# Two context attentions: the row sums of the softmax made in the spare half of each value tile, and divided through 32 transposed columns

## The chip, the cores and the metric

The kernel is one program on one core of a Trainium2 chip. The core has a matmul engine (PE; its weight loads are shown apart as PEld), three elementwise engines (DVE is VectorE, ACT is ScalarE, POOL is GpSimd) and a queue that only issues DMAs (SP). PE writes into PSUM, a memory of eight banks of 512 float32 columns by 128 partitions; the other engines read it from there. Each engine works through its own list in order and waits on semaphores for the others. The metric is the device time of one execution in microseconds.

## The reference

The program is a decoder of four layers over x of 8 sequences x 256 tokens x 256 features, with twelve stages; after each stage x is added to the stage's output and normalised. Two of the twelve (the second stage of layers 2 and 3, called stages 7 and 10 here) attend from x to a context of 77 rows per sequence, with 16 heads of width 16:

```python
q = (x @ Wq + bq).reshape(b, l, H, D).transpose(0, 2, 1, 3)
k = (context @ Wk + bk).reshape(b, s, H, D).transpose(0, 2, 1, 3)
v = (context @ Wv + bv).reshape(b, s, H, D).transpose(0, 2, 1, 3)
attn = jnp.einsum('bhld,bhsd->bhls', q, k) / jnp.sqrt(jnp.float32(D))
attn = jax.nn.softmax(attn, axis=-1)
out = jnp.einsum('bhls,bhsd->bhld', attn, v)
out = out.transpose(0, 2, 1, 3).reshape(b, l, E)
return out @ Wp + bp
```

Both have this form (the second with its weights transposed). All in float32.

## The kernel before

`cross16` builds both stages. Everything of a stage is pipelined over i = 0 to 11, with one sequence b entering at each i from 0 to 7, and the order of the work is written out by hand in the loop `for i in range(B + 4)` of each engine. For one sequence the steps are: queries (L296); scores of each half of the tokens, with the tokens on the partitions (L324), whose row maxima DVE takes (L504); the maxima transposed (L333) and sent by a DMA into one row of the padded queries; scores again, now with the 77 context rows on the partitions (L347, minus the maximum by that row), in two groups t = 0 and 1 of eight heads; their exponentials by ACT (L458); the product with the values (L361), for each t; the division (L511 and L513); the output projection (L377); residual sum and statistics (L520, L523, L526), the normalisation (L532), and x transposed for the next stage (L386, copied by ACT at L468).

Both kinds of scores use the same four banks, S.R. So within one i the sequence of their users is fixed: scores of the first half, maxima, scores of the second half, maxima, transposed scores t = 0, exponentials, transposed scores t = 1, exponentials, and then the next i. On PE the product of sequence i - 2, t = 1, stands between the two halves of the scores, and the product of sequence i - 1, t = 0, between the last transposed scores of i and the first scores of i + 1.

The heads' outputs are 16 wide, while PE writes 32 partitions for one group of columns of the array. So two heads share 32 partitions: v2 holds each head's values in one half of 32 columns (half s) and zeros in the other, and the two heads of a pair are added up in one bank, S_num. The row sums go the same way into a second bank, S_den, by a product with `ones2`, a tile that has ones in one half and zeros in the other (L365). Each matmul in float32 shows as two records in the trace, so a product of 8 matmuls is "x16". DVE takes the reciprocal of all of S_den (512 columns) and multiplies.

`keep_warm` (L212) issues matmuls whose result nobody reads, in places where PE has little to do; in these stages at i = 0 to 2 and from i = 10 on.

Of the kernel before, what the change touches and what calls it, by code (L numbers as in the profile page):

```python
# [12 lines left out]
ALU = mybir.AluOpType  # L13
ACT = mybir.ActivationFunctionType
AX = mybir.AxisListType

P = 128
B = 8
T = 256
# [8 lines left out]
CTX = 77  # L28
EPS = 1e-5
MASKED = -1e30  # L30
BANK = 512
# [23 lines left out]
def columns(parts):  # L55

    at, out = 0, {}
    for name, n in parts:
        out[name] = (at, n)
        at += n  # L60
    return out


CONST = columns([("ident", 128), ("causal", 128), ("causal_t", 128), ("block", 128), ("tri", 128), ("ones", 128),
                 ("steps", 256), ("past", 256), ("iota", 16), ("neg_half", 16), ("half", 64), ("row", 1),
                 ("head", HT), ("line_head", H), ("even", 1), ("odd", 1), ("sel", 3 * H), ("count", P)])
# [24 lines left out]
def part(image, table, name, chunks=None):  # L91

    at, n = table[name]
    v = image[:, at:at + n]
    return v.rearrange("p (c n) -> p c n", c=chunks) if chunks else v
# [93 lines left out]
def prefetch(nc, S, sp, k):  # L189

    if k < len(PACK):
# [8 lines left out]

Marks = namedtuple("Marks", "setup pads v_sb v_full k_full k_sb k_dma q_full q_sb q_dma s_full max_done neg_full neg_sb "
                            "neg_dma st_full exp_done pv_full attn_ready y_full yn_ready yt_full xt_done ln_stat "
                            "rstd_ready xres_ready y_read c_in c_stat c_rstd cn_ready cnt_sb first_done x_done xa_done xd_done xa_full "
                            "xd_full t_full pt_dve pt_act o_full rec_ready rows_ready recb_sb lat_stat lat_rstd lat_ready spare_free qb_done yb_done qa_full qd_full ya_full "
                            "yd_full feat_ready kg_ready line_ready lam_exp "
                            "setup_bc g_done prod_done state_done state_used diag_done odd_full odd_sb d_done raw_sb")
# [8 lines left out]
def settle(engine, mark, total):  # L215

    engine.wait_ge(mark, total)
    engine.sem_inc(mark, -total)
# [12 lines left out]
def cross16(nc, S, k, scale, first):  # L231
# [4 lines left out]
    W, TB, M = S.arena[k % 2], PACK[k], S.marks  # L236
    used = sum(n for _, n in TB.values())
    NK = B * CTX
    with ExitStack() as ctx:
        def sb(name, shape, dt=F32):  # L240
            return ctx.enter_context(nc.sbuf_tensor(f"{name}_{k}", shape, dt))

        v2 = W[:, used:used + B * H * 32].rearrange("p (b h m) -> p b h m", b=B, h=H)
        k_pad = W[:, used + B * H * 32:used + B * H * 32 + 4 * NK].rearrange("p (c n) -> p c n", c=4)
        prob_t = sb("prob_t", [P, C, 4, 2, T])
# [4 lines left out]
        rec = sb("rec", [P, C * T])  # L250
        attn_t = sb("attn_t", [P, 2, C, T])
# [2 lines left out]
        bst = sb("bst_own", [P, 2, TT, 6])  # L254
        mv = sb("mv_own", [P, 2, TT, 2])
        rstd = sb("rstd_own", [P, 2, TT])
        ones2 = sb("ones2", [P, 2, 32])
        bq_s = sb("bq_s", [P, C])
        S_q, S_y, S_num, S_den = S.T[:, 0, :], S.T[:, 1, :], S.O[:, 0, :], S.O[:, 1, :]

        def bank(j):
            return S.R[:, j // 2, j % 2 * BANK:(j % 2 + 1) * BANK]
# [24 lines left out]
        def _(pe):  # L287
# [64 lines left out]
            def product(b, t):  # L352
                pe.wait_ge(M.exp_done, 2 * b + t + 1)
                if t == 0:
                    if b == 0:
                        pe.wait_ge(M.v_sb, B // 2)
                    else:
                        pe.wait_ge(M.attn_ready, b)
                for s in range(2):
                    for j in range(4):  # L360
                        nc.tensor.matmul(S_num[32 * j:32 * j + 32, t * T:(t + 1) * T], v2[0:CTX, b, 8 * t + 2 * j + s, :],  # L361
                                         prob_t[0:CTX, t, j, s, :], start=(s == 0), stop=(s == 1), skip_group_check=True)
                for s in range(2):
                    for j in range(4):
                        last = nc.tensor.matmul(S_den[32 * j:32 * j + 32, t * T:(t + 1) * T], ones2[0:CTX, s, :],  # L365
                                                prob_t[0:CTX, t, j, s, :], start=(s == 0), stop=(s == 1), skip_group_check=True)
                if t == 1:
                    last.then_inc(M.pv_full, 1)

# [68 lines left out]
            settle(pe, M.neg_dma, 16 * B)  # L438
            settle(pe, M.exp_done, 2 * B)
            settle(pe, M.attn_ready, B)  # L440
            settle(pe, M.yn_ready, B)
            settle(pe, M.xt_done, B)

        @block.scalar
        def _(act):
            bk_even, bk_odd = part(W, TB, "bk_even"), part(W, TB, "bk_odd")
            even, odd = part(S.const, CONST, "even"), part(S.const, CONST, "odd")

            def queries(b):
                act.wait_ge(M.q_full, b + 1)  # L450
                for t in range(C):
                    last = nc.scalar.activation(q_pad[:, b % 3, 2 * t, :], S_q[:, t * T:(t + 1) * T], ACT.Identity,
                                                bias=bq_s[:, t:t + 1], scale=scale)
                last.then_inc(M.q_sb, 1)

            def exps(b, t):
                act.wait_ge(M.st_full, 2 * b + t + 1)
                nc.scalar.activation(prob_t[0:CTX, t, :, :, :].rearrange("p j s q -> p (j s q)"),  # L458
                                     S.R[0:CTX, :, :].rearrange("p a n -> p (a n)"), ACT.Exp).then_inc(M.exp_done, 1)

            def maxima(b):
                act.wait_ge(M.neg_full, b + 1)
                nc.scalar.activation(neg_t[:], S_q[0:H, 0:T], ACT.Copy).then_inc(M.neg_sb, 1)

            def transposed(b):
                act.wait_ge(M.yt_full, b + 1)
                y = S_y if b < B - 1 else S_q
                nc.scalar.activation(S.x_t[:, :, b * T:(b + 1) * T], y.rearrange("p (c t) -> p c t", c=C), ACT.Copy)\  # L468
                    .then_inc(M.xt_done, 1)

            act.wait_ge(S.weights_ready[k], 16)
            for t in range(C):
                act.wait_ge(M.k_full, t + 1)
                nc.scalar.activation(k_nat[:, t, :], S.R[:, t, 0:NK], ACT.Identity, bias=bk_odd[:, t:t + 1], scale=odd).then_inc(M.k_sb, 1)
            act.wait_ge(M.setup, 1)
            queries(0)
            for t in range(C):
                nc.scalar.activation(k_pad[:, 2 * t, :], S.R[:, t, 0:NK], ACT.Identity, bias=bk_even[:, t:t + 1], scale=even)\
                    .then_inc(M.k_sb, 1)
            for i in range(B + 4):  # L480
                if i + 1 < B:
                    queries(i + 1)
                if 0 <= i - 4 < B:
                    transposed(i - 4)
                if 0 <= i - 1 < B:
                    exps(i - 1, 0)
                if i < B:
                    maxima(i)
                if 0 <= i - 1 < B:
                    exps(i - 1, 1)  # L490
            settle(act, M.setup, 1)
            settle(act, M.q_full, B)
            settle(act, M.k_full, C)
            settle(act, M.st_full, 2 * B)
            settle(act, M.neg_full, B)
            settle(act, M.yt_full, B)

        @block.vector
        def _(dve):
            bv = part(W, TB, "bv")  # L500

            def maxima(b, qt):
                dve.wait_ge(M.s_full, 2 * b + qt + 1)
                nc.vector.tensor_reduce(neg_max[:, qt, :].rearrange("p (j c) -> p j c", j=4),  # L504
                                        S.R[:].rearrange("p a (e n) -> p (a e) n", e=2)[:, :, 0:4 * CTX]
                                        .rearrange("p j (c n) -> p j c n", c=4), AX.X, ALU.max, negate=True)\
                    .then_inc(M.max_done, 1)

            def quotient(b):
                dve.wait_ge(M.pv_full, b + 1)  # L510
                nc.vector.reciprocal(rec[:], S_den)  # L511
                dve.drain()
                nc.vector.tensor_tensor(attn_t[:, b % 2, :, :].rearrange("p c t -> p (c t)"), S_num, rec[:], ALU.mult)\  # L513
                    .then_inc(M.attn_ready, 1)

            def residual(b):
                dve.wait_ge(M.y_full, b + 1)
# [17 lines left out]

            dve.wait_ge(S.weights_ready[k], 16)
            nc.vector.tensor_scalar(bq_s[:], part(W, TB, "bq"), scale, None, ALU.mult).then_inc(M.setup, 1)
            nc.vector.memset(v2, 0.0)
            nc.vector.memset(ones2[:], 0.0)
            dve.drain()  # L540
            for s in range(2):
                nc.vector.memset(ones2[:, s, 16 * s:16 * s + 16], 1.0)

            def values(pair):
                dve.wait_ge(M.v_full, pair + 1)
# [26 lines left out]
            settle(dve, M.v_full, B // 2)  # L572
            settle(dve, M.s_full, 2 * B)
            settle(dve, M.pv_full, B)
            settle(dve, M.y_full, B)
            settle(dve, M.xres_ready, B)
            settle(dve, M.rstd_ready, B)
# [3903 lines left out]
def decoder(nc, dram, layers=range(12)):  # L4481

    with ExitStack() as ctx:
# [90 lines left out]
        with nc.Block() as block:  # L4574
# [33 lines left out]
            lambda k: moe_relu(nc, S, k),  # L4608
            lambda k: causal16(nc, S, k, D ** -0.5),
            lambda k: cross16(nc, S, k, DH16 ** -0.5, k == layers[0]),  # L4610
            lambda k: int8_product(nc, S, k),
            lambda k: selective_scan(nc, S, k),
# [120 lines left out]
```

## Time and profile before

| | |
|---|---|
| median of 3 runs | 3124.25 us (3118.69 to 3127.91) |
| the profiled execution, its own time | 3095.31 us |
| its span | 3093.5 us |
| PE busy | 2841.6 us, 92% of the span |
| DVE busy | 1909.1 us, 62% |
| ACT busy | 1199.2 us, 39% |
| mean granted clock of PE | 0.972 of full speed |
| stage 7 | about 2234 to 2371 us |
| stage 10 | about 2758 to 2891 us |

Times of rows are from the span's start. A timeline row gives start, duration, engine, line, operation, tiles, shape and count, and in brackets how long the engine had been idle before it and what released it. The duration of several merged instructions runs from the first start to the last end, and the ends on PE are modelled. The granted clock is either full (1.0, 2.4 GHz) or half (0.5, 1.2 GHz); a figure between them is a mean over the stretch.

### The profile page before, as it was taken

Reading aid. Unit: us, or ns where it says so; the run is one execution under the profiler, and the core shown is the slowest. Engines: PE = TensorE matmul, PEld = TensorE weight load, DVE = VectorE, ACT = ScalarE, POOL = GpSimd, SP = SyncE. Lnnn points to the kernel's source line nnn. Section 1 sums busy time; section 2 is a strip of 40 time slices with the busy share of each in tenths; the row PEclk is TensorE's granted clock in tenths of the full one; section 3 lists DMA queues with packets and bytes.
Section 4 is the critical chain, followed back from the end, with each engine's and each line's share of the span. In section 5 each row is a group of like instructions: output and inputs, shape, how many; then the busy total and the mean of one; then the engine's idle time right before and its main releaser. Section 6 shows DMA issues by size and latency. Waiting matters only on the chain. (4 is left out here: it accounts for less than half of the span.)

```text
span 3093.5 us, 55363 instructions
## 1 busy us (share of the span) xinstructions
PE 2841.6 (92%) x22416; PEld 1831.1 (59%) x22416; DVE 1909.1 (62%) x3404; ACT 1199.2 (39%) x2567; POOL 326.5 (11%) x460
## 2 busy tenths in 40 slices
PE   6999899999998978799999999989898899989898
PEld 3666456666666856466666667756565333346576
DVE  4666457777764335377777753345557999975532
ACT  1332245445542333254555432123232766634111
POOL 1111100000002700000000000100101000001232
PEclk9999999999999989899999999989999999999899
DMA  3001010000012231100000000000000000000241
GB/s 115 17 17 48 30 42 9 5 5 5 5 66 78 89 131 32 43 5 5 5 5 9 35 18 1 27 20 20 18 21 35 18 1 1 1 14 21 100 163 66
DMA packets 43418, 103.91 MB, mean 34 GB/s; under 512 B 4961, under 2 KB 32847, under 8 KB 39585
## 3 DMA queue, kind: packets, MB, share of 16 engines
q1 hardware_dynamic: 37377, 86.80, 8.1%
q0 software_dynamic: 5792, 13.59, 1.5%
q8 instruction: 182, 2.98, 0.4%
q14 instruction: 67, 0.55, 0.1%
HBM read 66.74 MB, written 19.07 MB: 28 GB/s over the span
## 5 line engine op out<-in xcount | busy, mean ns | idle before, releaser
L2388 ACT ACTIVATE prob<-R,neg_max 128x333 f32<-128x333 f32 x512 | 268.7, 538 | 184.1 <-DVE neg_max L2455 183.8
L3936 DVE TENSOR_TENSOR_SCAN arena<-arena,u 128x512 f32<-128x512 f32 x256 | 289.6, 1203 | 0.1
L2276 PEld LDWEIGHTS T<-const,prob 128*128 128x128 f32 (+1 forms) x1536 | 183.7, 143 | 82.1 <-DVE prob L2468 36.6
L2468 DVE TENSOR_TENSOR prob<-prob,rec 128x666 f32<-128x666 f32 x256 | 218.5, 853 | 20.2 <-issue 1.3
L2455 DVE TENSOR_REDUCE neg_max<-R 128x2 f32<-128x666 f32 x256 | 205.9, 846 | 35.2 <-PE R L2265 35.1
L2276 PE MATMUL T<-const,prob 128*128 128x128 f32 (+1 forms) x1536 | 210.9, 274 | 13.0 <-DVE prob L2468 10.7
L2395 ACT ACTIVATE prob_t<-T 128x384 f32<-128x384 f32 x256 | 125.8, 491 | 228.2 <-PE T L2276 222.1
L3867 ACT ACTIVATE arena<-delta,neg_a 128x510 f32<-128x510 f32 x256 | 175.4, 714 | 43.1 <-DVE arena L3936 42.0
L2461 DVE COPY prob_t<-T 128x384 f32<-128x384 f32 x256 | 142.3, 556 | 39.4 <-PE T L2276 13.0
L2195 PE MATMUL O<-keys_in,arena 128*128 128x333 f32 x512 | 164.8, 444 | 0.0
L3770 PE MATMUL R<-arena,diag 64*64 64x512 f32 x1024 | 134.7, 617 | 25.5 <-DVE arena L3936 25.4
L2191 PE MATMUL O<-keys_in,arena 128*128 128x256 f32 x512 | 127.7, 391 | 2.3 <-ACT keys_in L2361 2.3
L2202 PE MATMUL O<-arena,keys_in 128*128 128x512 f32 x256 | 125.1, 611 | 0.0
L2220 PE MATMUL O<-arena,attn_t 128*128 128x256 f32 x512 | 117.4, 382 | 1.0 <-DVE ysb L2438 1.0
L2191 PEld LDWEIGHTS O<-keys_in,arena 128*128 128x128 f32 x512 | 91.6, 189 | 37.1 <-issue 23.9
L944 DVE TENSOR_REDUCE neg_max<-R 128x8 f32<-128x2048 f32 (+1 forms) x24 | 55.0, 2292 | 94.5 <-PE R L721 94.5
L2220 PEld LDWEIGHTS O<-arena,attn_t 128*128 128x128 f32 x512 | 94.9, 190 | 19.8 <-issue 6.4
L2388 ACT ACTIVATION_READ_ACCUMULATOR prob<-R,neg_max 128x1 f32 x512 | 103.8, 203 | 0.0
L2195 PEld LDWEIGHTS O<-keys_in,arena 128*128 128x128 f32 x512 | 87.7, 191 | 24.0 <-issue 1.0
L2293 PE MATMUL O<-prob_t,v 128*64 128x256 f32 (+1 forms) x768 | 98.5, 392 | 1.3 <-DVE prob_t L2461 1.3
L2293 PE MATMUL O<-prob_t,arena 128*64 128x256 f32 (+1 forms) x768 | 97.2, 388 | 0.0
L3770 PEld LDWEIGHTS R<-arena,diag 64*64 64x64 f32 x1024 | 29.3, 133 | 112.9 <-DVE arena L3936 78.6
(597 smaller groups left out, 5390.1 us busy)
## 6 DMA issues: line engine op xcount, KB each, us to landing
w<-w_dram SPq DMA_DIRECT2D x16, 1024.0 KB, 7.0
arena<-pack_dram SPq DMA_DIRECT2D x2, 4100.0 KB, 15.2
q_pad<-q_pad SPq DMA_DIRECT2D x24, 224.0 KB, 2.7
arena<-pack_dram SPq DMA_DIRECT2D x4, 1284.0 KB, 6.5
arena<-pack_dram SPq DMA_DIRECT2D x1, 4896.0 KB, 14.6
slots_in<-x_nat SPq DMA_DIRECT2D x2, 2048.0 KB, 8.5
arena<-planes SPq DMA_DIRECT2D x8, 512.0 KB, 8.5
arena<-k_nat SPq DMA_DIRECT2D x16, 224.0 KB, 2.7
```

The source lines that it names most:

```text
L2191: last = nc.tensor.matmul(bank[:, h * T:(h + 1) * T], wq[:, c, (2 * i + h) * P:(2 * i + h + 1) * P], keys[:, c, CTX:XK], start=(c == 0), s ...
L2195: last = nc.tensor.matmul(bank[:, 0:XK], wkv[:, c, i * P:(i + 1) * P], keys[:, c, :], start=(c == 0), stop=(c == C - 1))
L2220: last = nc.tensor.matmul(bank[:, 0:D], attn_t[:, b % 2, c, i * P:(i + 1) * P], wo[:, c, :], start=(c == 0), stop=(c == HP - 1))
L2276: last = nc.tensor.transpose(S.T[0:n, i, kc * P:(kc + 1) * P], prob[:, g % 2, i, first:first + n], S.ident)
L2293: last = nc.tensor.matmul(S_o[XD * i:XD * (i + 1), 0:T], v[b % 2][0:n, kc, (2 * hp + i) * XD:(2 * hp + i + 1) * XD], prob_t[0:n, m % 2, i, ...
L2388: last = nc.scalar.activation(prob[:, g % 2, i, :], S.R[:, g % 2, i * BANK:i * BANK + XK], ACT.Exp, bias=neg_max[:, g % 2, i:i + 1], accum ...
L2455: nc.vector.tensor_reduce(neg_max[:, g % 2, :], S.R[:, g % 2, :].rearrange("p (i n) -> p i n", i=2)[:, :, 0:XK], AX.X, ALU.max, negate=Tru ...
L2461: nc.vector.tensor_copy(prob_t[:, m % 2, 0, :, qt * P:(qt + 1) * P], S.T[:, 0, 0:3 * P].rearrange("p (c q) -> p c q", c=3)).then_inc(M.pt_ ...
L2468: nc.vector.tensor_tensor(prob[:, g % 2, :, :], prob[:, g % 2, :, :], rec[:, g % 2, :].unsqueeze(2).to_broadcast([P, 2, XK]), ALU.mult)\
L3770: last = nc.tensor.matmul(sums(i, a)[to:to + HB, :], diag[rows, i % CT, n + a, :], state[rows, (q + a) % HELD, :], start=(a == 1 and n == ...
L3867: nc.scalar.activation(decay[:, q % DEEP, :].rearrange("p (b t) -> p b t", b=PAIR)[:, :, 1:T], delta[:, i % 2, :].rearrange("p (b t) -> p ...
L3936: nc.vector.tensor_tensor_scan(state[:, q % HELD, :], decay[:, q % DEEP, :], u[:, i % 2, :], 0.0, ALU.mult, ALU.add)\
```

## The change

Both heads of a pair no longer share a bank. v2 is filled with ones in place of zeros, so that each head's tile of 32 columns has its values in one half and ones in the other. The even head of a pair writes to one bank (S_one) and the odd head to the other (S_two), each by one matmul with no accumulation. On 32 partitions a bank then has 16 rows of the head's weighted values and 16 equal rows of its sums. `ones2` and the matmuls of L365 are gone: a product is 8 matmuls, not 16.

Putting the two heads together takes more steps on the elementwise engines. ACT copies S_one to SBUF, with `even` as a scale that sets the partitions of the sums to zero (`halves`). DVE transposes both banks in blocks of 32 x 32, adds the odd heads to ACT's copy (a scalar_tensor_tensor with the mask `odd`), takes the reciprocal of 32 columns, one for each block and bank, of the transposed tile, transposes these back with each repeated 16 times, and multiplies. PE may write the banks again after the sum (semaphore sums_read), where it had to wait for the whole division (attn_ready).

```diff
@@ product @@
                     if b == 0:
                         pe.wait_ge(M.v_sb, B // 2)
                     else:
-                        pe.wait_ge(M.attn_ready, b)
-                for s in range(2):
+                        pe.wait_ge(M.sums_read, b)
+                for s, sums in enumerate((S_one, S_two)):
                     for j in range(4):
-                        nc.tensor.matmul(S_num[32 * j:32 * j + 32, t * T:(t + 1) * T], v2[0:CTX, b, 8 * t + 2 * j + s, :],
-                                         prob_t[0:CTX, t, j, s, :], start=(s == 0), stop=(s == 1), skip_group_check=True)
-                for s in range(2):
-                    for j in range(4):
-                        last = nc.tensor.matmul(S_den[32 * j:32 * j + 32, t * T:(t + 1) * T], ones2[0:CTX, s, :],
-                                                prob_t[0:CTX, t, j, s, :], start=(s == 0), stop=(s == 1), skip_group_check=True)
+                        last = nc.tensor.matmul(sums[32 * j:32 * j + 32, t * T:(t + 1) * T], v2[0:CTX, b, 8 * t + 2 * j + s, :],
+                                                prob_t[0:CTX, t, j, s, :], start=True, stop=True, skip_group_check=True)
@@ scalar engine @@
+            def halves(b):
+                act.wait_ge(M.pv_full, b + 1)
+                if b >= 1:
+                    act.wait_ge(M.sums_read, b)
+                nc.scalar.activation(own[:], S_one, ACT.Copy, scale=even).then_inc(M.halves_sb, 1)
             for i in range(B + 4):
+                if 0 <= i - 2 < B:
+                    halves(i - 2)
                 if i + 1 < B:
                     queries(i + 1)
@@ vector engine @@
             def quotient(b):
                 dve.wait_ge(M.pv_full, b + 1)
-                nc.vector.reciprocal(rec[:], S_den)
-                dve.drain()
-                nc.vector.tensor_tensor(attn_t[:, b % 2, :, :].rearrange("p c t -> p (c t)"), S_num, rec[:], ALU.mult)\
-                    .then_inc(M.attn_ready, 1)
+                nc.vector.transpose(turned[:, 1, :], S_two)
+                dve.wait_ge(M.halves_sb, b + 1)
+                nc.vector.transpose(turned[:, 0, :], S_one)
+                shares = attn_t[:, b % 2, :, :].rearrange("p c t -> p (c t)")
+                nc.vector.scalar_tensor_tensor(shares, S_two, odd, own[:], ALU.mult, ALU.add).then_inc(M.sums_read, 1)
+                sums = turned[:].rearrange("p s n -> p (s n)")[:, 16:2 * BANK - 16].rearrange("p (s n) -> p s n", s=2)[:, :, 0:BANK - 31:32]
+                dve.drain()
+                nc.vector.reciprocal(inverse[:].rearrange("p n s -> p s n"), sums)
+                dve.drain()
+                nc.vector.transpose(rec[:].rearrange("p (n s m) -> p n s m", s=2, m=16), inverse[:].unsqueeze(3).to_broadcast([P, 16, 2, 16]))
+                dve.drain()
+                nc.vector.tensor_tensor(shares, shares, rec[:], ALU.mult).then_inc(M.attn_ready, 1)
@@ set-up @@
-            nc.vector.memset(v2, 0.0)
-            nc.vector.memset(ones2[:], 0.0)
-            dve.drain()
-            for s in range(2):
-                nc.vector.memset(ones2[:, s, 16 * s:16 * s + 16], 1.0)
+            nc.vector.memset(v2, 1.0)
+            dve.drain()
```

PE, stage 10, one pass of the loop in the middle of the pipeline (i = 4), before:

```order
L324 MATMUL R<-arena,q_pad 128x77 x16
L361 MATMUL O<-prob_t,arena 32x256 x8
L365 MATMUL O<-prob_t,ones_7 32x256 x8
L324 MATMUL R<-arena,q_pad 128x77 x16
L296 MATMUL T<-x_t,arena 128x256 x4
L386 MATMUL T<-const,x_nat 128x128 x4
L347 MATMUL R<-q_pad,arena 77x256 x8
L377 MATMUL T<-arena,attn_t 128x256 x4
L333 MATMUL T<-const,neg_max 16x128 x2
L347 MATMUL R<-q_pad,arena 77x256 x8
L361 MATMUL O<-prob_t,arena 32x256 x8
L365 MATMUL O<-prob_t,ones_7 32x256 x8
```

Now, the same pass (L324 of before is now L326, L361 is L363, and so on):

```order
L326 MATMUL R<-arena,q_pad 128x77 x16
L363 MATMUL O<-prob_t,arena 32x256 x8
L326 MATMUL R<-arena,q_pad 128x77 x16
L298 MATMUL T<-x_t,arena 128x256 x4
L384 MATMUL T<-const,x_nat 128x128 x4
L349 MATMUL R<-q_pad,arena 77x256 x8
L375 MATMUL T<-arena,attn_t 128x256 x4
L335 MATMUL T<-const,neg_max 16x128 x2
L349 MATMUL R<-q_pad,arena 77x256 x8
L363 MATMUL O<-prob_t,arena 32x256 x8
```

Two groups of 8 matmuls have gone; nothing else has moved on PE.

DVE, the same stage, the division in one pass, now (before, L511 RECIPROCAL of 128x512 and L513 TENSOR_TENSOR of 128x512 stood in this place, after the same two TENSOR_REDUCE):

```order
L519 STREAM_TRANSPOSE turned<-O 128x512
L521 STREAM_TRANSPOSE turned<-O 128x512
L523 SCALAR_TENSOR_TENSOR attn_t<-O,const,own 128x512
L526 RECIPROCAL inverse<-turned 128x2x16
L528 STREAM_TRANSPOSE rec<-inverse 128x512
L530 TENSOR_TENSOR attn_t<-attn_t,rec 128x512
L536 TENSOR_TENSOR ysb_own<-T,xres_own 128x512
```

Six instructions stand where two did. On ACT one more (L468 of the new kernel, own<-O, 128x512) stands ahead of the two copies of the queries in each pass from i = 2 to 9.

## Rows read from the trace of the kernel before

**Rows 1.** The page, busy time of the engines.
```profile
PE 2841.6 (92%) x22416; PEld 1831.1 (59%) x22416; DVE 1909.1 (62%) x3404; ACT 1199.2 (39%) x2567; POOL 326.5 (11%) x460
```

**Rows 2.** Groups by line and shape, PE: busy us, mean ns of one.
```profile
L365 PE MATMUL O<-prob_t,ones 77*32 77x256 f32 x512 | 33.5, 379 | 0.0
```

**Rows 3.** Timeline of stage 7, one pass of the loop (i = 6).
```profile
2321.37 1.07 PE L361 MATMUL O<-prob_t,arena 77*32 77x256 f32 x16
2321.50 1.44 DVE L504 TENSOR_REDUCE neg_max<-R 128x16 f32<-128x1232 f32 x1 [2.64 <-PE R L324]
...
2322.26 1.05 PE L365 MATMUL O<-prob_t,ones 77*32 77x256 f32 x16
...
2323.24 1.13 PE L324 MATMUL R<-arena,q_pad 16*128 16x77 f32 x32
...
2325.80 3.35 DVE L511 RECIPROCAL rec<-O 128x512 f32<-128x512 f32 x1
...
2329.22 0.69 DVE L513 TENSOR_TENSOR attn_t<-O,rec 128x512 f32<-128x512 f32 x1
...
2329.83 0.68 DVE L520 TENSOR_TENSOR ysb_own<-T,xres_own 128x512 f32<-128x512 f32 x1
...
2331.09 1.87 ACT L458 ACTIVATE prob_t<-R 77x2048 f32<-77x2048 f32 x1 [0.69 <-PE R L347]
...
2331.84 1.05 PE L365 MATMUL O<-prob_t,ones 77*32 77x256 f32 x16
...
2333.11 1.13 PE L324 MATMUL R<-arena,q_pad 16*128 16x77 f32 x32 [0.22 <-ACT prob_t L458]
...
2334.29 1.44 DVE L504 TENSOR_REDUCE neg_max<-R 128x16 f32<-128x1232 f32 x1 [2.64 <-PE R L324]
```

**Rows 4.** Stretches: us, busy (count) of PE, PEld, DVE, ACT, POOL, granted clock, DMA share, GB/s.
```profile
2270.20:2337.20 67.00, 65.06 (x994) 43.52 (x994) 44.60 (x49) 26.15 (x28) 9.24 (x16) 1.00 0.07 20
2337.20:2346.30 9.10, 8.03 (x46) 4.91 (x47) 6.84 (x6) 2.85 (x3) 0.00 (x0) 0.62 0.01 2
...
2860.40:2866.20 5.80, 4.73 (x46) 3.10 (x46) 5.72 (x4) 2.85 (x3) 0.00 (x0) 1.00 0.01 3
```

**Rows 5.** Timeline of stage 7 from the last maxima (i = 7) to the last transposes.
```profile
2337.23 1.44 DVE L504 TENSOR_REDUCE neg_max<-R 128x16 f32<-128x1232 f32 x1 [0.85 <-PE R L324]
...
2338.82 1.92 PE L347 MATMUL R<-q_pad,arena 17*77 17x256 f32 x16 [1.07 <-DVE neg_max L504]
...
2369.12 0.66 PE L386 MATMUL T<-const,x_nat 128*128 128x128 f32 x4
```

**Rows 6.** Timeline of stage 10, the same three instructions.
```profile
2860.41 1.44 DVE L504 TENSOR_REDUCE neg_max<-R 128x16 f32<-128x1232 f32 x1 [0.85 <-PE R L324]
...
2861.99 1.10 PE L347 MATMUL R<-q_pad,arena 17*77 17x256 f32 x16 [1.07 <-DVE neg_max L504]
...
2889.32 0.66 PE L386 MATMUL T<-const,x_nat 128*128 128x128 f32 x4
```

**Rows 7.** Timeline of stage 7, from i = 1 to i = 2.
```profile
2267.48 1.87 ACT L458 ACTIVATE prob_t<-R 77x2048 f32<-77x2048 f32 x1 [0.97 <-PE R L347]
...
2269.20 1.13 PE L212 MATMUL T<-ctx_t,const 128*128 128x512 f32 x2
2270.26 1.13 PE L324 MATMUL R<-arena,q_pad 16*128 16x77 f32 x32
```

**Rows 8.** Timeline of stage 10, the last division.
```profile
2877.36 1.57 DVE L532 TENSOR_SCALAR x_nat<-ysb_own,mv_own,rstd_own 128x256 f32<-128x256 f32 x2 [1.20 <-POOL rstd_own L597]
...
2879.22 3.36 DVE L511 RECIPROCAL rec<-O 128x512 f32<-128x512 f32 x1 [0.29 <-PE O L365]
```

**Rows 9.** Single lines: count, duration in ns (least/median/most), first and last start, form.
```profile
L468 ACT ACTIVATE x_t<-T x16: 598/599/600, 2301.5 to 2890.0; 128x512 f32<-128x512 f32 x16
L1925 DVE RECIPROCAL arena<-arena x8: 352/353/355, 45.6 to 279.8; 128x32 f32<-128x32 f32 x8
```

**Rows 10.** Groups by shape, 2200 to 2400 us: busy us, mean ns of one.
```profile
L3593 DVE TENSOR_SCALAR rows_i<-rows_i 128x512 f32<-128x512 f32 x5 | 2.1, 427 | 0.4
```

More of the change, by code:

```diff
@@ L202 @@
                             "neg_dma st_full exp_done pv_full attn_ready y_full yn_ready yt_full xt_done ln_stat "
-                            "rstd_ready xres_ready y_read c_in c_stat c_rstd cn_ready cnt_sb first_done x_done xa_done xd_done xa_full "
+                            "rstd_ready xres_ready y_read c_in c_stat c_rstd cn_ready cnt_sb first_done x_done xa_done xd_done halves_sb sums_read xa_full "
                             "xd_full t_full pt_dve pt_act o_full rec_ready rows_ready recb_sb lat_stat lat_rstd lat_ready spare_free qb_done yb_done qa_full qd_full ya_full "
@@ L256, in cross16 @@
         rstd = sb("rstd_own", [P, 2, TT])
-        ones2 = sb("ones2", [P, 2, 32])
+        own = sb("own", [P, BANK])
+        turned = sb("turned", [P, 2, BANK])
+        inverse = sb("inverse", [P, 16, 2])
         bq_s = sb("bq_s", [P, C])
-        S_q, S_y, S_num, S_den = S.T[:, 0, :], S.T[:, 1, :], S.O[:, 0, :], S.O[:, 1, :]
+        S_q, S_y, S_one, S_two = S.T[:, 0, :], S.T[:, 1, :], S.O[:, 0, :], S.O[:, 1, :]
         def bank(j):
@@ L440, in _ @@
             settle(pe, M.attn_ready, B)
+            settle(pe, M.sums_read, B)
             settle(pe, M.yn_ready, B)
@@ L500, in _ @@
             bv = part(W, TB, "bv")
+            odd = part(S.const, CONST, "odd")
             def maxima(b, qt):
@@ L574, in _ @@
             settle(dve, M.pv_full, B)
+            settle(dve, M.halves_sb, B)
             settle(dve, M.y_full, B)
```

## The prediction

> **What bounds the kernel now.** I read the page first, then the two stages as timelines, then stretches with the granted clock. The page has PE busy for 92% of the span [rows 1], which makes it look as if any matmul taken away were time gained. The removed matmuls, L365, are busy for 33.5 us in all [rows 2]. One pass of the loop says otherwise. It takes 2334.29 - 2321.50 = 12.79 us from one first maxima to the next [rows 3], and in it one chain through the shared banks S.R sets the time: scores, maxima on DVE, scores, maxima, transposed scores, exponentials on ACT, transposed scores, exponentials, scores. Both blocks of L365 stand beside a member of this chain that runs on another engine. The first (2322.26) lies beside the maxima of L504, which end at 2321.50 + 1.44 = 2322.94; the next scores start at 2323.24. The second (2331.84) lies beside ACT's exponentials, which end at 2331.09 + 1.87 = 2332.96; the next scores start at 2333.11, released by ACT. So PE is busy there, and nobody waits for what it does.
>
> DVE has the division (L511, 3.35 us, and L513, 0.69 us) after the second maxima, and waits 2.64 us for PE before the next pass [rows 3]. It is not the bound in the middle of a stage.
>
> The last thing to see is the clock. From 2270.20 to 2337.20, five full passes, PE is busy for 65.06 of 67.00 us at the full 2.4 GHz [rows 4]. Right behind, with the last maxima, PE had nothing to do for 1.07 us [rows 5], and in the stretch to 2346.30 the granted clock has a mean of 0.62: it fell to 1.2 GHz right after that gap. In stage 10 PE has the same gap of 1.07 us at the same place [rows 6], and the clock stays at 1.00 [rows 4]. So at this mix of work (scores on 16 rows of the array, a short idle time, transposes) a gap of about a microsecond brings the clock down in one of two cases. The price can be read off, as both stages run the same instructions: from L504 to the last L386 it is 2369.12 - 2337.23 = 31.89 us in stage 7 and 2889.32 - 2860.41 = 28.91 us in stage 10 [rows 5, 6], so one fall costs 2.98 us.
>
> **The change part by part.** All in the profiled execution, whose span is 3093.5 us and own time 3095.31.
>
> The matmuls that go. A block of L365 holds PE from 2322.26 to 2323.24, 0.98 us [rows 3].
> - Product t = 1, six passes a stage: without it the scores wait for DVE. After a release PE starts some 0.14 us later (2861.99 against 2860.41 + 1.44 = 2861.85 [rows 6]), so they start at 2323.08 and not 2323.24: 0.16 us each. What follows (queries, transposes, scores, projection) is PE's own unbroken work, so the gain is kept. 12 x 0.16 = 1.9 us.
> - Product t = 0 behind the last transposed scores: ACT sets the next scores, nothing. The exception is i = 1, where L212 stands behind it: the exponentials end at 2267.48 + 1.87 = 2269.35 and the scores start only at 2270.26 [rows 7]. Now 2269.49: 0.77 us in each stage, 1.5 us.
> - The end of a stage, where the last product and division are on the path. The last division starts at 2879.22, with the product before it and L532 (to 2877.36 + 1.57 = 2878.93) both just done [rows 8]. Both come earlier: the product by 0.98 us, L532 by what the earlier divisions and the earlier transposes give, which I take as 1.2 us.
>
> The division. Before: 3.42 to the start of the multiplication and 0.69, 4.11 us [rows 3]. Now six DVE instructions. An ordinary pass over 512 columns takes 0.69, and the next one starts 0.61 later (2329.22 to 2329.83) [rows 3]; a reciprocal of 32 columns takes 0.353 [rows 9]; a drain adds 0.07 (2325.80 + 3.35 to 2329.22). The transposes are in no row here. Their bounds are 0.43 us, the fastest pass over 512 columns [rows 10], and 3.35 us, the slowest (L511). I take 0.61 start to start, as they only move data. Sum: 3 x 0.61 for two transposes and the sum, 0.07, 0.35 + 0.07, 0.61 + 0.07, 0.69 = 3.7 us, 0.4 less. In the middle of a stage it is worth nothing, DVE has 2.64 us to spare; at the end of a stage it gives 0.4 once. With the 1.2 above 1.6 a stage, 3.2 us. With transposes at the lower bound 0.5 us less per division, at the upper bound see below.
>
> The Trainium skill has the transposes' price: "Vector Engine (DVE) Microarchitecture Reference", section 3.8, says the 32 x 32 reorder array is pipelined to one element per cycle and lane, so a transpose would cost what a copy does. No run so far shows it.
>
> ACT's copy of one bank: like L468, 0.60 us [rows 9]. It stands ahead of the queries' copies, at a time when ACT has just finished its exponentials and waits for PE. Behind it are the two copies that the DMA of the padded queries waits for, a whole pass ahead of their use. PE's queries come after the product on PE, so the copy is done before they are. Nothing.
>
> The waits. sums_read comes before attn_ready came, so PE waits no longer than before. ones2's memsets are gone from a start where DVE waits anyway. Nothing. No DMA is added or moved.
>
> So far -1.9 - 1.5 - 3.2 = -6.6 us.
>
> What the cover leaves behind. With L365 gone PE is idle in each pass twice: from about 2322.4 to 2323.1 beside the maxima, 0.6 us, and beside the exponentials from about 2332.0 to 2333.1, 1.1 us, with only 16-row scores and one small product in between. Both together exceed the gap of 1.07 us that brought the clock down in stage 7 [rows 5], and what lies between is thinner. It comes at the start of i = 3, 4, 5, 6 and 7 in both stages, and of i = 8 in stage 10 (stage 7 has that fall already): 11 places. The half clock would then lie on the part of the pass that is PE's alone (the second scores to the transposed scores t = 1, 2323.24 to about 2331), so nothing hides it. Bounds: no fall, 0; a fall at all 11, 11 x 2.98 = 33 us. I take 8 of 11, nearer to the upper end, as before one such gap in two was enough and now there are two in a row: 24 us.
>
> The Trainium skill has rules for both sides, in "TensorE: Matmul & The Clock Gate". Its section on HAM oscillation has the clock fall on long waits only, which would leave -6.6 us; the fall behind a 1.07 us gap speaks against it. The section on psum-queue depth-cycling says that micro-idles between groups of matmuls are enough for the clock to oscillate; the trace agrees once out of two.
>
> Sum: 24 - 6.6 = +17 us, about 3112 us in the profiled execution. That one is 29 us under the median of the runs (3124.25), so 3141 us for the median.
>
> **The rivals.**
> 1. The clock stays up. For it: stage 10 went through the same 1.07 us gap undisturbed, and five passes show not one fall. Against it: the new idle time is larger and returns in each pass. It gives -6.6 us: 3118.
> 2. PE's busy time is what counts, and the removed matmuls come off in full: -33.5 [rows 2] - 3 = 3088. For it: 92% busy, 65.06 of 67 us. Against it: both waits in rows 3 end on another engine. It would need the scores to start before the maxima or the exponentials are done.
> 3. DVE becomes the bound, through transposes that are slow on float32 or on PSUM. DVE has 2.64 us to spare in a pass; from a division of 4.11 + 2.64 = 6.75 us on it decides, that is transposes of 1.6 us each. At 3.35 each the division takes 12 us and a pass 5.2 us more: 12 passes, 62 us, 3186. For it: nothing in the trace shows such an instruction. Against it: plain passes over PSUM run at 0.69.
> Slower than before thus has two different ways, the clock and DVE; they can be told apart at once.
>
> **How the numbers follow.** What this kernel's measurement can tell from no change is about 0.3%, 9.4 us. Forecast, the clock falls in four passes or more (+5 to +33 us): 0.60, of which 0.52 is over +9.4. Rival 1: 0.24. Rival 2: 0.08. Rival 3: 0.08, nearly all of it over +9.4 us, 0.07. So slower 0.59, within 0.3% 0.29 (0.08 + 0.01 + 0.20 of rival 1), faster 0.12 (rival 2, and 0.04 of rival 1). The forecast's own range is 3129 to 3157. The whole range reaches to rival 1 with a little room, 3114, and to 3159.
>
> **What would show it.** In the profile after: L365's records gone; the scores behind the first product wait 0.1 to 0.2 us on DVE at a pass's start and PE's idle time before them is 0.6 us, and 1.1 us before those released by ACT; the division 3.7 us from first transpose to end; the granted clock of the middle of both stages clearly under 1.00, with passes of 15 to 16 us where it fell and of 12.6 where not. A clock of 1.00 in both stages makes rival 1 right. A pass of 10.8 us at full clock would be rival 2, a DVE without idle time before the first maxima rival 3. I am wrong if stages 7 and 10 together are not longer by 5 us or more, or if they are but at full clock.

## The result and the profile after

The changed kernel takes 3154.0 us (median of 7 runs, 3145.71 to 3168.41), the kernel before 3118.69 us (median of 7, the first three among them). The ratio is 1.0105, with a 95% interval of 1.0088 to 1.0122: slower by 1.05%, some 33 us. The forecast was slower, by 17 us. The profiled execution of the kernel before, 3095.31 us, on which the prediction's rows rest, is shorter than each of these seven (3111.51 to 3127.91).

The page of the changed kernel, busy time of the engines, answers to [rows 1]. 512 matmul records are gone and PE is busy for 31 us longer:

```profile
PE 2872.9 (91%) x21904; PEld 1850.1 (59%) x21904; DVE 1903.8 (60%) x3462; ACT 1209.4 (38%) x2583; POOL 325.5 (10%) x460
```

The five passes from the first maxima of i = 2 to those of i = 7, before, as stretches (columns as in [rows 4]), stages 7 and 10:

```profile
2271.46:2334.29 62.83, 60.89 (x900) 40.49 (x899) 42.52 (x46) 26.15 (x28) 9.24 (x16) 1.00 0.08 22
2794.64:2857.47 62.83, 60.89 (x900) 40.48 (x899) 42.52 (x47) 26.15 (x28) 9.23 (x16) 1.00 0.07 22
```

And after:

```profile
2297.38:2372.79 75.41, 68.13 (x740) 45.70 (x740) 41.16 (x66) 29.79 (x33) 9.23 (x16) 0.77 0.06 18
2828.40:2903.34 74.94, 68.20 (x740) 45.77 (x740) 41.17 (x67) 29.78 (x33) 9.22 (x16) 0.77 0.06 18
```

160 records fewer on PE, 7 us more of PE's time, and a clock of 0.77 where it was 1.00. The same five passes take 12 us more in each stage. The whole stages, from their first instruction to their last, went from 135.7 to 148.2 us and from 129.9 to 143.6 us, 26.2 us together.

One pass of stage 7 after (timeline, i = 5 with the seam to i = 6) answers to [rows 3]. Lines: L363 the product, L457 the exponentials, L326 the scores, L512 the maxima, L298 the queries, L519 to L530 the division:

```profile
2338.53 1.07 PE L363 MATMUL O<-prob_t,arena 77*32 77x256 f32 x16
2338.66 1.87 ACT L457 ACTIVATE prob_t<-R 77x2048 f32<-77x2048 f32 x1 [0.69 <-PE R L349]
...
2340.68 1.13 PE L326 MATMUL R<-arena,q_pad 16*128 16x77 f32 x32 [1.08 <-ACT prob_t L457]
2341.74 1.94 PE L363 MATMUL O<-prob_t,arena 77*32 77x256 f32 x16
2341.87 1.44 DVE L512 TENSOR_REDUCE neg_max<-R 128x16 f32<-128x1232 f32 x1 [2.65 <-PE R L326]
...
2343.61 2.00 PE L326 MATMUL R<-arena,q_pad 16*128 16x77 f32 x32
...
2345.54 3.45 PE L298 MATMUL T<-x_t,arena 128*128 128x256 f32 x8
...
2347.04 0.70 DVE L519 STREAM_TRANSPOSE turned<-O 128x512 f32<-128x512 f32 x1
2347.67 0.67 DVE L521 STREAM_TRANSPOSE turned<-O 128x512 f32<-128x512 f32 x1
2348.26 0.71 DVE L523 SCALAR_TENSOR_TENSOR attn_t<-O,const,own 128x512 f32<-128x512 f32 x1
...
2349.06 0.35 DVE L526 RECIPROCAL inverse<-turned 128x32 f32<-128x32 f32 x1
...
2349.49 0.71 DVE L528 STREAM_TRANSPOSE rec<-inverse 128x512 f32<-128x512 f32 x1
...
2350.28 0.69 DVE L530 TENSOR_TENSOR attn_t<-attn_t,rec 128x512 f32<-128x512 f32 x1
...
2358.49 1.80 PE L326 MATMUL R<-arena,q_pad 16*128 16x77 f32 x32 [0.55 <-DVE neg_max L512]
```

PE waits 1.08 us for ACT, and after the next product 0.55 us for DVE where that product ran at full clock (2358.49). In the pass shown the granted clock falls to half at 2341.71, 1.0 us after the wait for ACT ended, and stays there for 6.8 us. The product then takes 1.94 us instead of 1.07, the scores 2.00 instead of 1.13, the queries 3.45 instead of 1.99. The scores and the queries are on the path in full, the product with what it sticks out beyond the maxima (0.2 us). DVE waits 2.65 us for PE before the maxima, as before.

The profiled execution after took 3149.04 us, 53.7 us more than the one before, and only 26.2 of it lie in the two stages. Whether the rest is an effect of the change is asked below, with a second and third trace of the kernel before (again, again_b).

### The profile page after: what moved, and what is told of

The parts are those of the page before. It is cut to its first block and busy times, and to the rows that moved or that the text cites. A ratio compares the mean times of both kernels' runs of the same rounds, so it can differ in the third digit from the quotient of the medians.

```text
span 3147.2 us, 54463 instructions
## 1 busy us (share of the span) xinstructions
PE 2872.9 (91%) x21904; PEld 1850.1 (59%) x21904; DVE 1903.8 (60%) x3462; ACT 1209.4 (38%) x2583; POOL 325.5 (10%) x460
## 5 line engine op out<-in xcount | busy, mean ns | idle before, releaser
L2409 ACT ACTIVATE prob_t<-T 128x384 f32<-128x384 f32 x256 | 125.5, 490 | 228.3 <-PE T L2290 222.3
L2205 PEld LDWEIGHTS O<-keys_in,arena 128*128 128x128 f32 x512 | 91.6, 189 | 37.1 <-issue 23.9
L3753 PE MATMUL T<-x_t,arena 128*128 128x512 f32 x192 | 95.2, 620 | 1.6 <-PEq L3489 1.1
```

Source lines behind the costliest of these rows:

```text
L2205: last = nc.tensor.matmul(bank[:, h * T:(h + 1) * T], wq[:, c, (2 * i + h) * P:(2 * i + h + 1) * P], keys[:, c, CTX:XK], start=(c == 0), s ...
```

## The experiments

A ratio is that of the medians of a kernel and of the kernel before, run side by side on one chip, with its 95% interval. The other columns are read from one profiled execution of each: "middle" is the time of the five passes above in stages 7 and 10, "clock" the granted clock in them, "stages" the two whole stages. The kernels of twice, before_less and filled ran on one chip, those of twice_t1, twice_t0, thin and filled_more on a second, before_more on a third.

| kernel | ratio | middle, us | clock | stages, us |
|---|---|---|---|---|
| before | 1 | 62.83, 62.83 | 1.00, 1.00 | 135.7, 129.9 |
| changed | 1.0105 (1.0088 to 1.0122) | 75.41, 74.94 | 0.77, 0.77 | 148.2, 143.6 |
| twice | 1.0007 (0.9989 to 1.0024) | 62.84, 62.85 | 1.00, 1.00 | 127.5, 132.0 |
| before_less | 1.0084 (1.0059 to 1.0109) | 75.26, 75.63 | 0.77, 0.77 | 146.8, 143.5 |
| filled | 0.9963 (0.9945 to 0.9981) | 61.67, 61.67 | 1.00, 1.00 | 131.4, 127.6 |
| twice_t1 | 1.0110 (1.0077 to 1.0143) | 78.23, 76.66 | 0.79, 0.81 | 146.8, 148.7 |
| twice_t0 | 1.0044 (1.0028 to 1.0059) | 72.92, 69.57 | 0.84, 0.88 | 136.9, 134.4 |
| thin | 1.0117 (1.0089 to 1.0144) | 80.61, 79.97 | 0.73, 0.74 | 154.7, 146.4 |
| filled_more | 0.9965 (0.9949 to 0.9981) | 61.67, 61.67 | 1.00, 1.00 | 125.5, 125.2 |
| before_more | 0.9952 (0.9934 to 0.9969) | 62.83, 62.84 | 1.00, 1.00 | 126.8, 126.1 |

**Is it PE's missing work, or the new work on DVE and ACT?** twice gives PE its work back and leaves the rest of the change in place:

```diff
+                for again in range(2 if True else 1):
-                for s, sums in enumerate((S_one, S_two)):
+                    for s, sums in enumerate((S_one, S_two)):
...
```

> The changed kernel, with every product on PE issued twice over (the second writes the same values into the same banks), so that PE has as many matmuls as before; DVE and ACT do the new division. Clock theory (PE's new idle time brings the clock down): the falls go, passes of the middle take 12.8 us at a clock of 1.00, stages 7 and 10 last 136 and 130 us as before, give or take a fall, and the time is that of before within 0.3%. Rival (the six DVE instructions and ACT's copy cost the time, through a wait or a port): passes stay at 15 to 16 us and the ratio at 1.010.

Measured: 3121.73 us, ratio 1.0007. The first row of its middle, in stage 7:

```profile
2298.36:2361.20 62.84, 60.89 (x900) 40.49 (x899) 41.07 (x66) 29.60 (x33) 9.24 (x16) 1.00 0.08 22
```

PE has its 900 records and 60.89 us again and the pass is back to 12.57 us on average, with all six DVE instructions and ACT's copy in it. So the added work costs nothing in the middle. before_less is the counterpart, the kernel before with PE's work taken away. Its last product with the values signals to DVE in place of the last matmul of the sums:

```diff
-                        nc.tensor.matmul(S_num[32 * j:32 * j + 32, t * T:(t + 1) * T], v2[0:CTX, b, 8 * t + 2 * j + s, :],
+                        last = nc.tensor.matmul(S_num[32 * j:32 * j + 32, t * T:(t + 1) * T], v2[0:CTX, b, 8 * t + 2 * j + s, :],
...
-                for s in range(2):
+                for s in range(2 if b == 0 else 0):
                     for j in range(4):
                         last = nc.tensor.matmul(S_den[32 * j:32 * j + 32, t * T:(t + 1) * T], ones2[0:CTX, s, :],
```

> The kernel before, with the sums' matmuls issued for sequence 0 only; the later sequences are divided by the sums of sequence 0, so this part of the computation is left out. DVE and ACT do what they did. Clock theory: as slow as the changed kernel, 7 or 8 falls in each stage, stages of about 148 and 143 us, ratio 1.008 to 1.010. Rival (new DVE and ACT work): as before, or faster by the 0.2% that PE no longer does.

Measured: 3146.57 us, ratio 1.0084, and

```profile
2292.03:2367.29 75.26, 69.08 (x756) 46.26 (x755) 42.89 (x47) 26.37 (x28) 9.24 (x16) 0.77 0.06 18
```

This is the slow middle again, 0.15 us off in stage 7 and 0.69 us in stage 10 (75.63 against 74.94), with the same clock of 0.77 and without one instruction of the new division. The two together settle that the loss is the matmuls' absence.

**Can it be had back?** filled puts other matmuls into the two places, with 128 rows and into a bank that is free there:

```diff
+            def filler(ready, n):
+                pe.wait_ge(M.neg_sb, ready)
+                nc.tensor.matmul(S_q[:, 0:n], S.ident, S.ctx_t[:, 0, 0:n], start=True, stop=True)
...
                 if 0 <= i - 2 < B:
                     product(i - 2, 1)
+                if 3 <= i < B:
+                    filler(i, T)
...
                     product(i - 1, 0)
+                if 2 <= i < B:
+                    filler(i + 1, BANK)
```

> The changed kernel with one matmul of 128 rows that nobody reads in each of the two idle places of a pass: 256 columns before the second scores, 512 columns before the next pass's first scores. Clock theory: clock 1.00 in the middle of both stages, passes of 12.6 us, ratio to the kernel before 0.998, so 1.1 to 1.2% under the changed one. Rival (DVE and ACT work): no better than the changed kernel, 1.010.

Measured: 3112.09 us, ratio 0.9963, where 0.998 was expected. The middle in stage 7:

```profile
2295.51:2357.18 61.67, 60.13 (x758) 37.97 (x759) 41.06 (x66) 29.57 (x33) 9.23 (x16) 1.00 0.08 22
```

Its timeline there, the fillers (L370) before the second scores and before the next pass:

```profile
2345.50 0.70 PE L370 MATMUL T<-ctx_t,const 128*128 128x256 f32 x2
...
2346.13 1.13 PE L326 MATMUL R<-arena,q_pad 16*128 16x77 f32 x32
...
2354.84 1.13 PE L370 MATMUL T<-ctx_t,const 128*128 128x512 f32 x2
...
2356.00 1.13 PE L326 MATMUL R<-arena,q_pad 16*128 16x77 f32 x32
```

All scores of the middle run at full clock, and the passes of i = 4 to 6 take 12.56 us, against 12.79 before.

**Which of the two gaps?** twice_t1 and twice_t0 repeat one product each, and leave one gap:

```diff
-                for again in range(2 if True else 1):
+                for again in range(2 if t == 1 else 1):     (twice_t1; t == 0 in twice_t0)
```

> The changed kernel with only product t = 1 issued twice, the one beside the maxima; the idle 1.1 us beside ACT's exponentials stays. Clock theory in its strong form (a gap of 1.1 us that comes back in each pass is enough by itself, as the one in stage 7 before): falls in most passes, ratio to before 1.004 to 1.008. Weak form (both gaps are needed together): clock 1.00 in the middle, ratio 0.999.

> The changed kernel with only product t = 0 issued twice, the one beside ACT's exponentials; the idle 0.6 us beside the maxima stays. Both forms of the clock theory: no falls in the middle, since 0.6 us is less than any gap behind which the clock fell here, passes of 12.6 us, ratio 0.998. If it falls all the same, the sum of work taken away counts and not the length of the gap.

Measured: ratios 1.0110 and 1.0044, and in the middle of stage 7 (twice_t1, then twice_t0):

```profile
2270.51:2348.74 78.23, 72.01 (x820) 47.56 (x820) 41.17 (x66) 29.59 (x33) 9.22 (x16) 0.79 0.06 17
```

```profile
2267.77:2340.69 72.92, 68.29 (x820) 45.76 (x819) 41.18 (x66) 29.68 (x33) 9.22 (x16) 0.84 0.06 18
```

With the gap of 1.1 us alone the clock falls in nearly every pass, and the time is as long as with both gaps, longer than the strong form had expected (1.004 to 1.008). Part of that is the test itself: the product that is issued twice takes 3.64 us where it runs at half clock (2300.40 in twice_t1), so a fall costs more there. The gap of 0.6 us alone brings the clock down too, to 0.84 and 0.88. In the stage 7 of twice_t0, the clock falls at 2298.74, during the scores behind it:

```profile
2298.15 1.51 PE L326 MATMUL R<-arena,q_pad 16*128 16x77 f32 x32 [0.55 <-DVE neg_max L513]
```

Both forms of the theory said it would not, since no gap that short had a fall behind it in the kernel before. So the length of a gap was not the right measure.

**Is it idle time at all?** thin is filled with the fillers on 16 rows of the array:

```diff
-                nc.tensor.matmul(S_q[:, 0:n], S.ident, S.ctx_t[:, 0, 0:n], start=True, stop=True)
+                nc.tensor.matmul(S_q[:, 0:n], S.ident[0:16, :], S.ctx_t[0:16, 0, 0:n], start=True, stop=True)
```

> The kernel called filled, with both fillers on 16 rows of the array in place of 128, and as long in time. If idle time on PE is what brings the clock down, this is as good as filled: clock 1.00, passes of 12.6 us, ratio 0.996. If it matters what PE does in that time, and not only that it does something, falls come back: passes of 15 to 16 us and a ratio of 1.003 to 1.008.

Measured: 3131.79 us, ratio 1.0117. The middle in stage 7, and one seam of it in the timeline:

```profile
2267.43:2348.04 80.61, 79.21 (x758) 52.39 (x758) 41.19 (x67) 29.57 (x33) 9.23 (x16) 0.73 0.06 17
```

```profile
2292.47 1.07 PE L363 MATMUL O<-prob_t,arena 77*32 77x256 f32 x16
...
2293.47 1.12 PE L370 MATMUL T<-ctx_t,const 16*128 16x512 f32 x2
2294.62 1.88 PE L326 MATMUL R<-arena,q_pad 16*128 16x77 f32 x32
2296.43 1.93 PE L363 MATMUL O<-prob_t,arena 77*32 77x256 f32 x16
```

This is the strongest case. PE is busy for 79.21 of 80.61 us and idle for 1.40, less than in filled (1.54), and the clock is the lowest of all. The filler takes 1.12 us at full clock, as the wide one did (1.13). The instruction count and the columns are the same, only 16 rows stand in place of 128, and the middle is 19 us longer. The passes take 16.2 to 17.2 us from i = 3 on and the ratio is 1.0117, both above what was expected (15 to 16 us, 1.003 to 1.008); the fillers themselves run at half clock in part, on the path. So the "idle time" theory falls. What PE does in these places decides, not that it does something. Which property of the work counts beside its rows (its columns, its share of the time) was not separated.

**How good can it get, and what is the change worth?** filled_more also fills the gaps that the kernel before has at the start of a stage and at i = 7; before_more has those fillers in the kernel before. At i = 0 the kernel before has no keep_warm; it has them at i = 1 and 2 and from i = 10 on:

```diff
-                if 0 < i < 3:
-                    keep_warm(nc, S, S_y, 1)
+                if i < 3:
+                    keep_warm(nc, S, S_y, (1, 2, 1)[i])
...
                 if i == 1:
-                    keep_warm(nc, S, S_y, 1)
+                    keep_warm(nc, S, S_y, 2)
...
+                if i == B - 1:
+                    filler(i, BANK)
```

> The kernel called filled, and fillers also in the gaps that the kernel before has: one or two matmuls of 512 columns more at i = 0 and 1, and one of 512 columns before the transposed scores of i = 7, where PE waits 1.07 us for the maxima. Clock theory: the falls at i = 0 and 1 (two in stage 7, one in stage 10) and at i = 7 go, 3 us each less 1 us for the fillers at the start, so 3 to 8 us under filled, a ratio of 0.994. Rival: those falls come from the long wait for the queries' DMA and stay; then it is filled plus 2 us.

The stages are 8.3 us shorter than filled's, at the upper end of the 3 to 8 us expected, but the ratio was 0.9965 and not 0.994, the same as filled's. As filled had run on another chip, both ran again side by side:

> filled once more, now beside filled_more on one chip. Its stages were 131.4 and 127.6 us, the time outside them 2855. Expected: ratio 0.996 again and the same stages within one fall (3 us).

> filled_more once more. Its two stages were 8.3 us shorter together than filled's, yet its ratio to the kernel before was the same. If the stages' gain is real and the first ratio was noise of the other stages, it is now 6 to 10 us under filled in the same call, a ratio of 0.993 to 0.994. If something outside the stages gives it back, the two are alike.

> The kernel before (sums by their own matmuls, the long division), with only the fillers of filled_more at i = 0 and 1 and before the transposed scores of i = 7. It tells what the change itself is worth once the clock is kept up in both. Expected from the passes: filled_more's six passes of 11.95 to 12.56 us against 12.18 to 12.79 give 1.3 us a stage, and the ends of the stages 2 us each: before_more is 6 to 7 us above filled_more and 3 to 7 us under the kernel before.

Measured: filled_b 3118.08 us, ratio 0.9968 (0.9951 to 0.9984); filled_more_b 3111.54 us, 0.9963 (0.9947 to 0.9980); before_more 3112.06 us, 0.9952 (0.9934 to 0.9969). filled_more is 6.5 us under filled, the expected size, but the intervals overlap, the ratio of 0.993 to 0.994 did not come, and this is not settled. The stages were 134.8 and 126.5 us for filled_b and 127.2 and 126.5 for filled_more_b, so their starts move by several us between executions of one kernel. In both, the clock also came down once in stage 7 outside the places of the new fillers: at i = 1 of filled_b for 23.9 us (its middle took 64.09 us), and at i = 2 of filled_more_b for 3.4 us (63.31), behind a wait of 0.55 us. So "clock 1.00 in the middle" holds for both stages of the first execution of each, and for stage 10 of the second.

before_more, expected 6 to 7 us above filled_more and 3 to 7 us under the kernel before, is level with filled_more and 13.9 us under the kernel before. The middles differ as expected, 62.83 against 61.67 us; part of the gain is lost at the end of the stages. Of the whole stages 2.1 us are left (250.7 against 252.9 us for the two), and none with the second trace of filled_more (253.7). Stretches from the end of the last scores of i = 7 on PE to the end of stage 7, filled_more and then before_more:

```profile
2338.35:2369.96 31.61, 27.30 (x198) 16.20 (x195) 23.34 (x47) 12.24 (x12) 6.65 (x12) 0.89 0.01 2
```

```profile
2355.42:2386.12 30.70, 27.05 (x260) 15.84 (x257) 24.36 (x35) 10.85 (x10) 6.66 (x12) 1.00 0.01 2
```

And the last division and projection (L379, L381) of each:

```profile
2355.12 1.07 PE L363 MATMUL O<-prob_t,arena 77*32 77x256 f32 x16 [0.99 <-ACT prob_t L467]
...
2358.56 6.18 PE L379 MATMUL T<-arena,attn_t 128*128 128x256 f32 x16 [0.78 <-ACT x_t L483]
...
2359.80 0.69 DVE L540 TENSOR_TENSOR attn_t<-attn_t,rec 128x512 f32<-128x512 f32 x1
```

```profile
2376.02 1.97 PE L381 MATMUL T<-arena,attn_t 128*128 128x256 f32 x8 [0.78 <-ACT x_t L474]
...
2378.15 0.69 DVE L519 TENSOR_TENSOR attn_t<-O,rec 128x512 f32<-128x512 f32 x1
...
2378.90 1.99 PE L381 MATMUL T<-arena,attn_t 128*128 128x256 f32 x8 [0.91 <-DVE attn_t L519]
```

The last division ends 2360.49 - 2338.35 = 22.1 us after the stretch's start in filled_more and 2378.84 - 2355.42 = 23.4 us in before_more, 1.3 us earlier. But there the clock falls once more (0.89) in filled_more, in stage 10 too, and in neither stage of before_more, and the two last projections take 6.18 us where 2 x 1.98 would do. The products at the end are half of what they were and have no filler; that this is the reason is likely but not shown, as a filler there was not tried. So with the clock kept up in both, the change is not shown to be worth anything: before_more is as good as filled_more and needs none of the new division.

**The time outside the stages.**

> The kernel before once more, unchanged, for a second trace. In the profiled executions the changed kernel is 53.7 us longer, but only 26.2 us of it lie in stages 7 and 10; the medians differ by 35. If the other 27.5 us are chance (where the clock falls in stages that the change doesn't touch), this trace has a span of about 3110 to 3120 us and the same 136 and 130 us in the two stages. If they belong to the change, it has 3093 again.

> The kernel before, unchanged, for a third trace. Stages of 136 and 130 to 133 us; the time outside them, 2828 and 2860 us in the first two traces, shows how far it moves by itself.

Measured: spans of 3128.5 and 3120.7 us, of which 2859.6 and 2859.2 lie outside the two stages. The first trace had 2827.9, the changed kernel's 2855.5. So the 27.6 us are no effect of the change: two of three traces of the kernel before have as much outside the stages as the changed kernel. They are not all chance from one execution to the next either. The four traces from one of the three chips (twice_t1, twice_t0, thin, filled_more) have 2826 to 2837 us outside the stages, the eight from the two others 2851 to 2868, and the medians of the kernel before on the three are 3103.17, 3120.13 and 3125.96 us. The first trace of the kernel before looks like one of the first group; on which chip it was taken is not on record. Spans of traces are therefore compared within one chip, or stage by stage. The stages themselves were 135.7 and 133.3, then 127.5 and 134.1 us: their starts (i = 0 to 2) differ by a fall or two from one execution to the next, their middles by nothing.

## Why the prediction was right, point by point

- **PE is busy but not waited for.** Right. The removed matmuls gave 0.23 us in a pass (12.79 to 12.56 in filled), 0.16 were expected, and not the 2 us that they were busy for. At i = 1 the expected 0.77 us came: without a fall, that pass takes 12.73 us in stage 7 of again_b and 11.95 in stage 10 of the changed kernel.
- **DVE and ACT are off the path.** Right (twice). The division takes 3.93 us from the first transpose to the end (2347.04 to 2350.97), 3.7 expected, 4.11 before. The transposes, which no row had shown, take 0.70, 0.67 and 0.71 us on float32, from PSUM as from SBUF, like other passes over 512 columns (0.69). With that the price in the Trainium skill, "Vector Engine (DVE) Microarchitecture Reference", section 3.8, agrees: one element per cycle and lane. ACT's copy takes 0.69, expected 0.60.
- **The idle time left behind.** Right: 0.55 and 1.08 us, 0.6 and 1.1 expected.
- **Its price: 24 us, 8 falls of 11 at 2.98 us each.** The direction and the place were right, this term was too small, in the number of falls and in the price of one. A fall came around the start of each of i = 3 to 7 in both stages, at all ten places that the prediction named there; its eleventh place, the wait behind the last maxima in stage 10 (its i = 8), lies inside the long fall of i = 7. Eight of the ten lie in the two middles with nearly all their length, and there they cost 13.74 + 13.27 = 27.0 us over filled's 61.67, or 3.4 us each: they lasted 6.8 or 10.2 us, while the one that 2.98 was read from lasted 6.8. The weight of one in two came from too few cases. In the three traces of the kernel before, the clock fell in or right behind the wait of 1.07 us at i = 7 in five of six stages; the stage 10 that the prediction read was the exception.
- **The sum.** The two stages grew by 26.2 us. That is also 11 x 2.98 - 6.6, and the two stages together have 11 more falls than before (8 against 3, 7 against 1), but the agreement is a coincidence. The middles account for 24.7 us, the stretches before them for -5.7 (at i = 1 of stage 10 a fall stayed away), and those behind them for +7.2: 0.7 in stage 7, and 6.5 in stage 10, where before had no fall and the changed kernel had three, one of them at i = 7. The falls at the very end (at 2396.32 in stage 7, at 2918.56 and 2928.80 in stage 10) were in no term.
- **The range.** The measured 3154.0 us lies in the forecast's own range of 3129 to 3157 partly by luck. The upper end takes 11 falls, 33 us, without the 6.6 us that the sum takes off. With them it would be 3150, and the measured time would lie above it.
- **Why it falls: idle gaps.** Wrong as a mechanism, though it gave the right sign. The text named the thin work between the gaps, but what it compared were lengths of gaps. twice_t0 falls with 0.55 us, and thin falls with PE busy for 98% of the time. The section of the Trainium skill on HAM oscillation ("TensorE: Matmul & The Clock Gate"), with its long waits, does not describe this, as the forecast said. The one on psum-queue depth-cycling, with micro-idles between groups of matmuls, fits the changed kernel but not thin, which has the falls without the idle time.
- **The end of a stage: 1.6 us each.** The size was right, the gain was not got. The division did end 1.3 us earlier (filled_more against before_more), and a fall of the clock at the same place took it back.
- **The reference point.** The forecast was set on a median of 3124.25; with seven runs it is 3118.69. The medians differ by 35 us, the two stages by 26.2 in one trace of each; with an interval of 27 to 38 us for the whole, some of the remaining 1 to 12 us is unexplained. The stages of the kernel before alone move by 7 us over its three traces (261.6 to 268.9 us), and the time outside them by more.

Rivals: the clock staying up (1) fell with the clock of 0.77; PE's busy time coming off in full (2) with filled; DVE as the bound (3) with twice.

## What to carry to other kernels

Before taking matmuls away, see whether anyone waits for them, and then what is left beside them. Where PE's remaining work in that place is thin, on few rows of the array, the removed work may have been what held the clock, and a matmul that nobody reads, on all 128 rows, can buy it back for nothing if it fits into the wait, as in filled. Judge such a place by the granted clock of the stretch, not by PE's busy share, which was 98% in the slowest variant here. And when a variant with fillers beats the old kernel, give the old kernel the same fillers before the change is credited with the gain.

## What the runs showed of the hardware

- The same filler in 16 rows and in 128 rows of the array takes the same 1.12 to 1.13 us, and the granted clock of the five passes is 0.73 with the one and 1.00 with the other.
- With the same matmuls taken away in two ways, the clock fell in nearly every pass, and the five passes took 75.41 and 74.94 us in the one, 75.26 and 75.63 in the other, against 62.83: 2.4 to 2.6 us more a pass.
- A wait of 1.07 us on PE, behind 16-row scores and one group of transposes and before 17-row scores, had a fall of the clock in it or right behind it in five of six stages of the same kernel (before, again, again_b), and one of 0.55 us had falls behind it in twice_t0 (clock 0.84 and 0.88).
- Removing work in a kernel made PE busier: in the five passes of stage 7, where before_less leaves out 144 matmul records and no instruction of the other engines, 60.89 to 69.08 us.
- A DVE transpose of 32 x 32 blocks over 128x512 float32 takes 0.67 to 0.71 us, from PSUM or from SBUF with a repeated source, against 3.35 us for a reciprocal of the same size.
